# A first product by 49 block products instead of seven, in groups of 2048 tokens

## The chip, the cores and the metric

The kernel runs on one core of one Trainium2 chip. The metric is the time of one execution on the device in microseconds (us). Three runs of the kernel before took 2756.13 to 2757.7 us, median 2757.11. The profiled execution is a run of its own and took 2755.91 us.

## The reference

`x` is 32 batches of 128 tokens with 2048 features, in float32. Two residual layers follow one another; each batch chooses its adapter by one id per layer.

```
# layer 0: dense weight for all batches, and a rank-16 adapter chosen per batch (8 adapters)
base  = einsum('bsi,oi->bso', x, W0) + bias
low   = einsum('bsi,bri->bsr', x, a[id0])
delta = einsum('bsr,bor->bso', low, b[id0])
x = x + base + scale[id0] * delta
# layer 1: a whole 2048 x 2048 weight chosen per batch out of 16
x = x + einsum('bij,bkj->bik', x, W1[id1])
```

Both layers are 4096 x 2048 x 2048 products in float32.

## The kernel before

Each float32 operand is split into two fp32r parts, `hi` (a rounding copy on ACT, line 574) and `lo` = value minus `hi` (a subtraction on DVE with both inputs in SBUF, line 710), and each product is three matmuls: hi·hi, hi·lo and lo·hi (lines 766, 767, 777 in the first product; 820 to 822 in the second). The residual is an identity matrix that POOL adds to the weights (lines 486 and 493).

The batches are sorted by their id of layer 1 on the chip. Four groups g of 1024 tokens (two halves of 512) go through both products one after the other. The first product of a group is done by seven block products k instead of eight, at one level, on quarters of weight and tokens: half of the outputs by half of the inputs, 8 tiles each way. For each k the operands are sums or differences of quarters. They are made in the ring `raw` of eight 4 KB tiles: SP loads the pieces (`raws_of` gives them), POOL adds them in place (line 476, 128x1024), eight sums of the weight fall to DVE (line 644). Sums of W0 are written to memory in group 0 and read back in groups 1 to 3, one sum of x is kept per group. A `W` block (g, k, o) is one output tile: 8 input tiles times three matmuls of 512 columns, 24 in all, into one of three PSUM banks in turn. DVE (for k = 0 ACT, line 543) takes the bank and adds it into up to two of the four result quarters `cb` (lines 687 to 704, 128x512 out of PSUM). So of DVE's large instructions some have two inputs in SBUF (line 710), and some have one in PSUM (lines 687 to 704).

`LA` blocks are the adapter's first product (16 matmuls), with the adapter's second product in the `W` blocks of k = 2, 3, 5 (line 775) and as `LB` after those of k = 6 (line 787).

The second product is streamed: per half, 512 output columns and 256 inputs there are three `S` blocks of 12, 6 and 6 matmuls, each with its tile of W1 (4 KB a partition, split as above). ACT copies the result out, SP stores it.

What sets the order: `plan_blocks` writes TensorE's order down. From it, with a price per block (`COST`, 0.2267 us a matmul), planned start and end times are summed, each split and eviction gets a key out of these times, and the sorted keys are the order on ACT, DVE, POOL and SP. Each engine then goes through its list in order and waits by semaphores. POOL's instructions stand in the order of the splits that they serve; SP issues every load and store, and a load into a ring place waits until the split of what lay there is done.

## Time and profile before

| | |
|---|---|
| three runs, median (lowest to highest) | 2757.11 us (2756.13 to 2757.7) |
| the profiled execution, its own time | 2755.91 us |
| its span in the profile | 2754.1 us |
| TensorE clock granted | 0.999 |
| busy: PE, DVE, ACT, POOL | 99%, 67%, 49%, 27% |
| DMA share of the span | 69% |

PE is TensorE's matmul side. The busy shares are unions of the recorded instructions of an engine over the span; an instruction that has begun and is held up is recorded as busy, so a mean over all instructions of a line mixes undisturbed and held ones.

### The profile page before, as it was taken

What the parts mean: (1) busy time and instruction counts of PE and PEld (TensorE: products, weight loads), DVE (VectorE), ACT (ScalarE), POOL (GpSimd) and SP (SyncE); (2) the same over time, 40 slices, a digit from 0 to 9 for tenths busy, and PEclk for the clock granted to TensorE, in tenths of its full rate; (3) what the DMA queues carried; (4) which work ended last, traced back from release to release, by engine and by line L of the source; (5) the groups of instructions that cost most, each with busy time, mean ns of one, the idle gap of its engine ahead of it and who ended that gap; (6) DMA issues with size and microseconds to landing.
All of it is one profiled execution on the core that took longest, in us unless ns stands there. A gap on an engine that the chain in (4) does not pass through costs nothing.

```text
span 2754.1 us, 34174 instructions
## 1 busy us (share of the span) xinstructions
PE 2713.4 (99%) x12042; PEld 2244.8 (82%) x12042; DVE 1836.7 (67%) x1631; ACT 1339.2 (49%) x1409; POOL 732.9 (27%) x589
## 2 busy tenths in 40 slices
PE   6999999999999999999999999999999999999999
PEld 5788888888888888888888888888888888888887
DVE  5766776866655657686656575768675656667865
ACT  3332355756533335576643232666664323366665
POOL 4435812411512111141251210113134122111421
PEclk9999999999999999999999999999999999999999
DMA  7858947666855435666794544899997554499997
GB/s 269 331 188 284 351 167 225 206 222 219 312 173 198 143 129 178 211 221 208 232 310 161 185 156 137 288 305 312 308 326 276 168 180 163 138 303 311 309 321 246
DMA packets 197627, 645.17 MB, mean 234 GB/s; under 512 B 23216, under 2 KB 33616, under 8 KB 197456
## 3 DMA queue, kind: packets, MB, share of 16 engines
q1 hardware_dynamic: 197456, 642.98, 68.6%
q8 instruction: 96, 1.57, 0.2%
q14 instruction: 75, 0.61, 0.1%
HBM read 651.28 MB, written 58.72 MB: 258 GB/s over the span
## 4 chain that ended last, share of the span: by engine, by line
PE 89%; POOL 3%; DMA 3%; DVE 3%; ACT 1%; issue 1%; SPq 0%; POOLq 0%; ACTq 0%; DVEq 0%
PE acc L820 16%; PE acc L821 16%; PE acc L822 16%; PE acc L766 13%; PE acc L777 13%; PE acc L767 13%; DMA raw<-w 3%; POOL raw L493 2%; PE acc L739 2%; DVE ws L710 1%; POOL raw L476 1%; PE acc L775 1%; DMA raw<-xt 0%; DVE ops L710 0%; ACT ws L574 0%
## 5 line engine op out<-in xcount | busy, mean ns | idle before, releaser
L710 DVE TENSOR_TENSOR ws<-raw,ws 128x1024 fp32r<-128x1024 f32 (+1 forms) x1008 | 1317.5, 1330 | 432.9 <-ACT ws L574 428.8
L574 ACT CAST ws<-raw 128x1024 fp32r<-128x1024 f32 (+1 forms) x1008 | 1027.9, 1044 | 1146.7 <-PE acc L777 519.0
L820 PE MATMUL acc<-ws,ops 128*128 128x512 f32 (+1 forms) x2048 | 799.0, 390 | 5.2 <-DVE ws L710 4.8
L821 PE MATMUL acc<-ws,ops 128*128 128x512 f32 (+1 forms) x2048 | 797.9, 390 | 0.0
L822 PE MATMUL acc<-ws,ops 128*128 128x512 f32 (+1 forms) x2048 | 797.9, 390 | 0.0
L766 PE MATMUL acc<-ops,ws 128*128 128x512 f32 x1792 | 702.1, 392 | 19.8 <-DVE ops L710 14.4
L777 PE MATMUL acc<-ops,ws 128*128 128x512 f32 x1792 | 700.9, 391 | 0.0
L767 PE MATMUL acc<-ops,ws 128*128 128x512 f32 x1792 | 699.8, 391 | 0.0
L493 POOL TENSOR_TENSOR raw<-raw,eye_s 128x128 f32<-128x128 f32 x384 | 351.6, 946 | 1261.3 <-DMA raw<-w 1261.3
L820 PEld LDWEIGHTS acc<-ws,ops 128*128 128x128 f32 x2048 | 384.6, 188 | 89.1 <-issue 6.5
L476 POOL TENSOR_TENSOR raw<-raw 128x1024 f32<-128x1024 f32 (+1 forms) x116 | 305.6, 2636 | 555.1 <-DMA raw<-xt 456.5
L822 PEld LDWEIGHTS acc<-ws,ops 128*128 128x128 f32 x2048 | 384.6, 188 | 79.5
L821 PEld LDWEIGHTS acc<-ws,ops 128*128 128x128 f32 x2048 | 384.7, 188 | 78.6
L766 PEld LDWEIGHTS acc<-ops,ws 128*128 128x128 f32 x1792 | 338.0, 189 | 88.0 <-DVE ops L710 14.6
L767 PEld LDWEIGHTS acc<-ops,ws 128*128 128x128 f32 x1792 | 337.9, 189 | 69.6
L777 PEld LDWEIGHTS acc<-ops,ws 128*128 128x128 f32 x1792 | 337.5, 188 | 67.7
L710 DVE TENSOR_TENSOR ops<-raw,ops 128x1024 fp32r<-128x1024 f32 x112 | 171.8, 1534 | 68.2 <-ACT ops L574 67.6
L574 ACT CAST ops<-raw 128x1024 fp32r<-128x1024 f32 x112 | 117.3, 1048 | 180.9 <-PE acc L777 85.6
L710 DVE TENSOR_TENSOR ops<-cb,ops 128x1024 fp32r<-128x1024 f32 x64 | 84.0, 1312 | 0.0
L486 POOL TENSOR_TENSOR raw<-raw,eye_s 128x128 f32<-128x128 f32 x80 | 68.4, 863 | 57.8 <-DMA raw<-w 56.4
L692 DVE SCALAR_TENSOR_TENSOR cb<-acc,bias_s,cb 128x512 f32<-128x512 f32 x32 | 24.0, 751 | 85.8 <-PE acc L777 85.8
L574 ACT CAST ops<-cb 128x1024 fp32r<-128x1024 f32 x64 | 67.1, 1048 | 13.8 <-PE acc L777 13.8
(61 smaller groups left out, 651.4 us busy)
## 6 DMA issues: line engine op xcount, KB each, us to landing
raw<-w SPq DMA_DIRECT2D x928, 512.0 KB
raw<-xt SPq DMA_DIRECT2D x176, 512.0 KB
raw<-w_sums SPq DMA_DIRECT2D x104, 512.0 KB
out<-ost SPq DMA_DIRECT2D x128, 256.0 KB, 6.0
w_sums<-raw SPq DMA_DIRECT2D x32, 512.0 KB, 5.3
x_sums<-raw SPq DMA_DIRECT2D x16, 512.0 KB, 4.2
raw<-x_sums SPq DMA_DIRECT2D x16, 512.0 KB
raw<-a SPq DMA_DIRECT2D x80, 64.0 KB
```

The costliest lines, as they stand in the source:

```text
L476: eng.tensor_tensor(b, b, a, ALU.subtract if step == "sub" else ALU.add).then_inc(s_pool, 1)
L486: eng.tensor_tensor(v, v, eye_s[:], ALU.add).then_inc(s_pool, 1)
L493: ins = eng.tensor_tensor(v, v, eye_s[:], ALU.add)
L574: ins = eng.copy(hi, src)
L710: ins = eng.tensor_tensor(lo, src, hi, ALU.subtract) if hi is not None else eng.tensor_copy(lo, src)
L739: ins = eng.matmul(acca[:], a_view(n)[:, t, :], ops[:, h + t, w, :], start=(i % 2 == 0 and t == 0 and w == 0), stop=(i % 2 == 1 and t == H ...
L766: eng.matmul(acc, wh, xh, start=(t == 0), stop=False)
L767: eng.matmul(acc, wh, xl, start=False, stop=False)
L777: ins = eng.matmul(acc, wl, xh, start=False, stop=(t == HT - 1))
L820: eng.matmul(acc, yh, wh, start=begin, stop=False)
L821: eng.matmul(acc, yh, wl, start=False, stop=False)
L822: ins = eng.matmul(acc, yl, wh, start=False, stop=end)
```

## The change

There are now two groups of 2048 tokens (four quads q of 512), and the first product has two levels. The outer seven products k are on halves as before; each is again done by seven products s, whose operands are 512 inputs by 512 outputs by 512 tokens. A block `W` (g, k, s, b) is two output tiles of 4 input tiles each, again 24 matmuls of 512 columns, into a pair of PSUM banks; there are 7 x 7 x 2 = 98 blocks per group, where one level on 1024 tokens had 56. The pairs of s = 2, 3 and 4 go on adding into the pair that s = 1 began, and s = 6 into that of s = 5 (`more`), so that the sums of a chain build up in PSUM; DVE (ACT for four of seven s at k = 0 and 3) takes the pair after every s, 128x1024, and the next block into that pair waits for it. Two pairs alternate.

Operands: for each k, four quarters r of each side in two halves h lie in SBUF as 128x1024 tiles, in ten places a side. Level-one sums (`Xform`, `Wform`) are added there by POOL, 512 columns at a time, from four small tiles `temps`: two per tile of x for k = 2, one for k = 3, 4 and 5; in group 0 also one per tile of the weight for k = 3, 5 and 6. Level-two sums are made by POOL out of these, in place: T3, T2, T4, T1 of x and S3, S2, S4, S1 of the weight, each for both h and every k, 128x1024. The quarters of k+1 are loaded into the places of k as its splits finish. DVE makes the weight sum of k = 2 at the start, in eight times two additions. Every operand of s is split, 14 tiles of x and 14 of weight per k, 128x1024 each. The finished result quarters go to memory (`keep`, `ystore`) and some come back (`back`, and `Y` loads); POOL adds kept ones in (`join`, 128x1024, eight at k = 3 and eight at k = 5). `LA` blocks are 16 of 8 matmuls per group; `LB` is apart from the `W` blocks, in bursts of four 256-column matmuls, each followed by two additions of 512 columns on DVE. Three operand slots of the weight instead of four. The second product has the same blocks as before, two groups of 768; its ring has ten places. POOL and SP now have lists of their own, sorted by planned times that `Plan` works out: it gives an addition of 128x1024 2.7 us, a load 3.5 us and a split 2.8 us, and does not let the instructions of an engine queue behind one another.

```diff
--- before.py
+++ after.py
@@ -11,229 +11,500 @@
...
-HT = 8
 G = 4
-NG = 4
-NQ = 8
+NG = 2
+NQ = 4
...
+X_ROLE = (0, 1, 4, 3, 0, 1, 2)
+W_ROLE = (0, 1, 4, 2, 3, 1, 0)
+X_NEXT = (4, 3, 0, 1, 2)
+W_NEXT = (4, 2, 3, 1, 0)
+X_QUARTER = ((1, 0), (0, 0), (1, 1), (0, 1))
+W_QUARTER = ((0, 1), (0, 0), (1, 0), (1, 1))
+BLOCK = ((0, 0), (0, 0), (0, 1), (1, 1), (1, 0), (1, 1), (0, 1))
+EARLIER = {1: 0, 5: 3, 6: 2}
+FINAL = {(0, 0): 1, (0, 1): 6, (1, 1): 5, (1, 0): 4}
+LORA_K = (0, 1, 3, 6)
+LORA_S = (0, 1, 3, 6)
+COPY_S = (0, 2, 3, 4)
+FINAL_K = (1, 4, 6)
+LB_AT = {(0, 0, 0): (1, ((2, 1), (3, 0))), (0, 1, 0): (2, ((1, 0), (1, 1))),
+         (0, 0, 1): (2, ((2, 1), (3, 0))), (0, 1, 1): (3, ((1, 0), (1, 1))),
+         (1, 0, 0): (4, ((2, 1), (3, 0))), (1, 1, 0): (5, ((1, 0), (1, 1))),
+         (1, 1, 1): (5, ((2, 0), (2, 1))), (1, 0, 1): (5, ((3, 0), (3, 1)))}
+LB_LATE = [(c, i, j) for c in (2, 3) for j in range(2) for i in range(2)]
 
 
 def plan_blocks():
...
+        for k in range(NP):
+            for s in range(NP):
+                for b in range(2):
+                    blocks.append(("W", g, k, s, b))
+                    if b == 0 and k in LORA_K and s in LORA_S:
+                        blocks.append(("LA", g, k, s))
+                    if (k, s, b) in early:
+                        blocks.append(("LB", g) + early[k, s, b])
+        for q in range(NQ):
             for kc in range(C1):
                 for u in range(NU):
                     for j in range(3):
-                        blocks.append(("S", g, h, kc, u, j))
-                        if held:
-                            blocks += held
-                            held = []
...
+def form_steps(side, g, k):
+    if side == "X":
+        return (0, 0, 2, 1, 1, 1, 0)[k]
+    return 1 if g == 0 and k in (3, 5, 6) else 0
+
+
+def saved_here(side, g, k):
+    return k == 2 if side == "X" else g == 0 and k in (3, 5, 6)
+
+
+def eye_here(g, k):
+    return k in (0, 4) or (g == 0 and k in (3, 5))
+
+
...
+        ready, free = [], []
+        for h in range(2):
+            slot = 2 * at[g, k][r] + h
+            before[g, k, r, h] = saves[slot]
+            fill[slot] += 32 if side == "X" and k in (0, 1, 2, 6) else 16
+            landed[g, k, r, h] = fill[slot]
+            t = when[h]
+            if (g, k) == (0, 0):
+                t = 18.0 + 0.01 * r + 0.001 * h if side == "X" else 0.01 * r + 0.001 * h
+            elif (g, k, side) == (0, 2, "W"):
+                t = max(t, self.early_done + 6.0)
+            self.sync.append((t, (side + "load", g, k, r, h)))
+            t += LOAD
+            for step in range(form_steps(side, g, k)):
+                done = t
+                for l in range(2):
+                    use = (side, g, k, r, h, l, step)
+                    done = max(self.take_temp(use, 1, t - LOAD + 0.2 * l, 1), done)
+                    what = (side + "form", g, k, r, h, l, step)
+                    self.pool.append((done, what))
+                    done += ADD / 2
+                    self.give_temp(use, 1, done, ("pool", what))
+                t = done
+            if side == "W" and r in (1, 3) and eye_here(g, k):
+                self.pool.append((t, ("eye", g, k, r, h)))
+                t += 1.2
+            ready.append(t)
+            if saved_here(side, g, k):
+                saves[slot] += 16
...
+            for h in range(2):
+                t3 = max(x_ready[2][0][h], x_ready[3][1][h])
+                t2 = max(t3 + ADD, x_ready[1][0][h], x_free[4][h])
+                xs[h] = (t3, t2)
+                self.pool += [(t3, ("T3", g, k, h)), (t2, ("T2", g, k, h))]
+                s3 = max(w_ready[1][0][h], w_ready[2][1][h])
+                s2 = max(s3 + ADD, w_ready[3][0][h], w_free[4][h])
+                wsum[h] = (s3, s2)
+                self.pool += [(s3, ("S3", g, k, h)), (s2, ("S2", g, k, h))]
+            have_x = {0: x_ready[0][0], 1: x_ready[1][0], 2: [xs[h][1] + ADD for h in range(2)],
...
+                for h in range(2):
+                    key = max(free + 0.3 + 3.0 * h, have_x[s][h])
+                    self.splits.append((key, "X", (g, k, s, h)))
+                    done.append(key + SPLIT)
+                xd[s] = done
+                if s < 2:
+                    for h in range(2):
+                        t = max(xs[h][1] + ADD, done[h], x_ready[s][1][h])
+                        self.pool.append((t, ("T4" if s == 0 else "T1", g, k, h)))
...
+        def pair_of(s, b):
+            return pair[((1, 2), (0, 1), (0, 1), (0, 1), (0, 1), (2, 0), (2, 0))[s][b]]
...
+                    z21, z11, z22, z12, v = (x_view(g, k, r, h) for r in range(5))
+                    if kind == "T3":
+                        wait_x(eng, g, k, 2, h)
+                        wait_x(eng, g, k, 3, h)
+                        wait_saved(eng, "X", g, k, 3, h)
+                        ins = eng.tensor_tensor(z12, z22, z12, ALU.subtract)
+                    elif kind == "T2":
+                        eng.wait_ge(s_pool, pool_no["T3", g, k, h])
+                        wait_x(eng, g, k, 1, h)
+                        wait_x_free(eng, g, k, 4, h)
+                        ins = eng.tensor_tensor(v, z12, z11, ALU.add)
+                    elif kind == "T4":
+                        eng.wait_ge(s_pool, pool_no["T2", g, k, h])
+                        eng.wait_ge(s_lo, number["X", g, k, 0, h] + 1)
+                        wait_saved(eng, "X", g, k, 0, h)
+                        ins = eng.tensor_tensor(z21, z21, v, ALU.subtract)
+                    else:
+                        eng.wait_ge(s_pool, pool_no["T2", g, k, h])
+                        eng.wait_ge(s_lo, number["X", g, k, 1, h] + 1)
+                        wait_saved(eng, "X", g, k, 1, h)
+                        ins = eng.tensor_tensor(z11, z22, v, ALU.subtract)
+                    ins.then_inc(s_pool, 1)
...
+                    if kind == "Xform" and k in (2, 3):
+                        ins = eng.tensor_tensor(t, t, other, ALU.add if step else ALU.subtract)
+                    elif kind == "Wform" and k == 5:
+                        ins = eng.tensor_tensor(t, t, other, ALU.add)
+                    else:
+                        ins = eng.tensor_tensor(t, other, t, ALU.subtract)
...
+                elif kind == "join":
+                    _, g, k, i, j, b = what
+                    m = 2 * (2 * i + j) + b
+                    if k == 3:
+                        eng.wait_ge(s_keep[m], 16 * (g + 1))
+                        wait_ev(eng, g, 3, FINAL[i, j], b)
+                        wait_ev(eng, g, 2, FINAL[i, j], b)
+                    else:
+                        eng.wait_ge(s_back[m], 16 * (g + 1))
+                        wait_ev(eng, g, 5, FINAL[i, j], b)
...
+            elif kind == "X":
+                g, k, s, h = index
+                m = 4 * ((NP * k + s) % 2)
+                v = x_view(g, k, X_ROLE[s], h).rearrange("p (l t c) -> p l t c", l=2, t=4)
+                hi, lo = (ops[:, m:m + 4, w, 256 * h:256 * h + 256].rearrange("p t (l c) -> p l t c", l=2)
+                          for w in range(2))
...
+                if what == "copy":
+                    g, k, s, b = index
+                    i, j = BLOCK[s]
+                    if k == 0 and g:
+                        eng.wait_ge(s_lo, max(number["Y", g - 1, 3, u] for u in range(NU)) + 1)
+                    if k == 3:
+                        eng.wait_ge(s_y[2 * (2 * i + j) + b], 32 * g + 16)
+                    eng.wait_ge(s_mm, at["W", g, k, s, b] + 1)
+                    eng.copy(cube(1 if k == 0 else 0, i, j, b), pair_of(s, b)[:]).then_inc(s_copy, 1)
...
+                if what == "ev":
+                    g, k, s, b = index
+                    i, j = BLOCK[s]
+                    which = 0 if k in (1, 3, 4) else 1
+                    t = cube(which, i, j, b)
+                    if s in EARLIER:
+                        wait_ev(eng, g, k, EARLIER[s], b)
+                    elif k == 1:
...
+                    eng.wait_ge(s_mm, at["W", g, k, s, b] + 1)
+                    source = cube(1, i, j, b) if k == 1 and s not in EARLIER else t
+                    eng.tensor_tensor(t, pair_of(s, b)[:], source, ALU.add).then_inc(s_ev, 1)
                     continue
...
+                    _, g, k, s, b = blk
+                    n, m = (14 * k + 2 * s + b) % NWS0, 4 * ((NP * k + s) % 2)
+                    if b == 0:
+                        eng.wait_ge(s_lo, max(number["X", g, k, s, h] for h in range(2)) + 1)
...
+                    if s == 0 and k:
+                        wait_ev(eng, g, k - 1, 6 if b else 4, 0 if b else 1)
+                    elif s == 0 and g:
+                        eng.wait_ge(s_ev1, out_no(g - 1, NQ * C1 - 2, 3 if b else 1) + 1)
+                    elif s == 1 and b:
+                        wait_ev(eng, g, k, 0, 0)
+                    elif s == 1 and k:
+                        wait_ev(eng, g, k - 1, 6, 1)
+                    elif s == 1 and g:
+                        eng.wait_ge(s_ev1, out_no(g - 1, NQ * C1 - 1, 1) + 1)
+                    elif s == 5 and b:
+                        wait_ev(eng, g, k, 4, 0)
+                    elif s == 5:
+                        wait_ev(eng, g, k, 0, 1)
+                        for burst in bursts:
...
+                    more = s in (2, 3, 4, 6)
+                    for o in range(2):
+                        acc = pair_of(s, b)[:, 512 * o:512 * o + 512]
+                        for t in range(4):
+                            c = P * (4 * o + t)
+                            wh, wl = ws0[:, n, 0, c:c + P], ws0[:, n, 1, c:c + P]
+                            xh, xl = ops[:, m + t, 0, :], ops[:, m + t, 1, :]
+                            eng.matmul(acc, wh, xh, start=(t == 0 and not more), stop=False, skip_group_check=more)
+                            eng.matmul(acc, wh, xl, start=False, stop=False, skip_group_check=more)
+                            ins = eng.matmul(acc, wl, xh, start=False, stop=(t == 3), skip_group_check=more)
                     ins.then_inc(s_mm, 1)
                 else:
```

## Rows read from the trace of the kernel before

**Rows 1.** The page: span, and busy us (share) and instructions of each engine.
```profile
span 2754.1 us, 34174 instructions
...
PE 2713.4 (99%) x12042; PEld 2244.8 (82%) x12042; DVE 1836.7 (67%) x1631; ACT 1339.2 (49%) x1409; POOL 732.9 (27%) x589
```
**Rows 2.** TensorE's waits: engine, line, released by: us in total, times, longest.
```profile
PE acc L766 <- DVE ops L710: 14.4, 1, 14.4
PE acc L766 <- DVE ws L710: 5.2, 4, 1.7
PE acc L820 <- DVE ws L710: 4.8, 5, 1.6
```
**Rows 3.** Windows: from:to, length, busy us (instructions) per engine, TensorE clock, DMA share, GB/s.
```profile
24.00:362.00 338.00, 329.89 (x1458) 271.71 (x1458) 231.56 (x210) 109.51 (x113) 182.45 (x96) 0.99 0.79 282
362.00:711.00 349.00, 347.53 (x1534) 287.24 (x1533) 253.72 (x208) 220.93 (x233) 82.34 (x85) 1.00 0.65 215
711.00:1040.00 329.00, 329.00 (x1478) 273.11 (x1477) 193.77 (x191) 113.26 (x120) 72.53 (x50) 1.00 0.53 182
```
**Rows 4.** The chain that ended last: start us, us, what.
```profile
759.09 3.63 PE acc L739 x16
...
944.58 7.25 PE acc L739 x32
```
**Rows 5.** Instructions grouped by form: count | busy us, mean ns | idle before.
```profile
L710 DVE TENSOR_TENSOR ws<-raw,ws 128x1024 fp32r<-128x1024 f32 x992 | 1303.8, 1337 | 431.4 <-ACT ws L574 427.6
...
L766 PE MATMUL acc<-ops,ws 128*128 128x512 f32 x1792 | 702.1, 392 | 19.8 <-DVE ops L710 14.4 <-DVE ws L710 5.2
...
L476 POOL TENSOR_TENSOR raw<-raw 128x1024 f32<-128x1024 f32 x112 | 300.5, 2684 | 524.6 <-DMA raw<-xt 456.5 <-DMA raw<-w 66.2 <-POOL raw L476 0.4
...
L710 DVE TENSOR_TENSOR ops<-raw,ops 128x1024 fp32r<-128x1024 f32 x112 | 171.8, 1534 | 68.2 <-ACT ops L574 67.6
...
L702 DVE TENSOR_TENSOR cb<-acc,cb 128x512 f32<-128x512 f32 x32 | 22.1, 691 | 75.2 <-PE acc L777 75.2
...
L476 POOL TENSOR_TENSOR raw<-raw 128x512 f32<-128x512 f32 x4 | 5.2, 1292 | 30.5 <-DMA raw<-a 30.5
```
**Rows 6.** Timeline of DVE, 198 to 209 us: start, us, engine, line, instruction.
```profile
199.19 1.21 DVE L710 TENSOR_TENSOR ops<-raw,ops 128x1024 fp32r<-128x1024 f32 x1
200.32 3.42 DVE L710 TENSOR_TENSOR ws<-raw,ws 128x1024 fp32r<-128x1024 f32 x1
204.22 0.75 DVE L692 SCALAR_TENSOR_TENSOR cb<-acc,bias_s,cb 128x512 f32<-128x512 f32 x1 [0.48 <-PE acc L777]
204.89 2.62 DVE L710 TENSOR_TENSOR ws<-raw,ws 128x1024 fp32r<-128x1024 f32 x1
```
**Rows 7.** Timeline of POOL in the same stretch.
```profile
199.85 2.81 POOL L476 TENSOR_TENSOR raw<-raw 128x1024 f32<-128x1024 f32 x1 [5.04 <-DMA raw<-w]
202.74 1.32 POOL L486 TENSOR_TENSOR raw<-raw,eye_s 128x128 f32<-128x128 f32 x1
204.03 2.40 POOL L476 TENSOR_TENSOR raw<-raw 128x1024 f32<-128x1024 f32 x1
```
**Rows 8.** Timeline: the first matmul of the first product.
```profile
23.67 0.80 PE L766 MATMUL acc<-ops,ws 128*128 128x512 f32 x1 [14.44 <-DVE ops L710]
```
**Rows 9.** SP's timeline: the first loads of weight and of x.
```profile
2.60 0.90 SPq L423 DMA_DIRECT2D raw<-w  x2
11.80 0.88 SPq L431 DMA_DIRECT2D raw<-xt  x2
```
**Rows 10.** Windows again: the first stretch after that matmul.
```profile
24.00:75.00 51.00, 49.90 (x210) 40.74 (x210) 32.84 (x31) 16.99 (x22) 31.94 (x16) 1.00 0.85 310
```
**Rows 11.** The page's DMA issues: count, KB each, median us from issue to landing.
```profile
out<-ost SPq DMA_DIRECT2D x128, 256.0 KB, 6.0
...
x_sums<-raw SPq DMA_DIRECT2D x16, 512.0 KB, 4.2
```
**Rows 12.** The chain that ended last again: two loads in it.
```profile
49.23 5.69 DMA raw<-xt
...
99.54 7.35 DMA raw<-w
```

More of the change, by code:

```diff
@@ new lines, in x_piece, with w_piece @@
+            def x_piece(g, iq, quad, lane):
+                src = xt[bass.ds(order(NQ * g + quad, 0)[lane], 1), iq]
+                return src.rearrange("a p n -> (a p) n")
+            def w_piece(k, r, h):
+                ro, co = {0: (0, 0), 1: (0, 1), 4: (1, 1)}[k]
+                ri, ci = W_QUARTER[r]
+                return w0[2 * ro + ri, 2 * co + ci, h]
+            constants = False
+            for _, what in plan.sync:
+                kind = what[0]
+                if not constants and kind == "Xload":
+                    constants = True
@@ L506, in split_views @@
             if kind == "Y":
[L507 to L516 removed]
+                g, q, u = index
```

1465 lines of the change are left out of this document (939 added, 526 removed).

## Prediction

> **What bounds the kernel now.** I read the busy shares first: TensorE 2713.4 us of a span of 2754.1 [rows 1]. Its waits come to little: 14.4 us for the first operands, then pieces of about 5 us [rows 2]. The windows say the same by stage: 329.89 of 338 us in group 0's first product, 347.53 of 349 in its second, 329.00 of 329 in group 1's first [rows 3]. So TensorE is the bound and everything else fits beneath it; a change that takes matmuls out pays only while that stays so. The question is what the others need per block afterwards.
>
> Two prices of TensorE: 16 matmuls of 512 columns in 3.63 us and 32 in 7.25 [rows 4], 0.2267 us each. A W block is 24 of them, 5.44 us.
>
> **What POOL and DVE do to each other** decides this case. The means are 2684 ns for POOL's 128x1024 addition and 1337 or 1534 for DVE's lo subtraction [rows 5]; the timelines show what is in them. DVE's subtraction from 199.19 ends at 200.40. POOL's addition had begun at 199.85 and ends at 202.66, 2.26 after that. DVE's next began at 200.32 and ends at 203.74, 1.08 after POOL. POOL's 128-wide addition ends at 204.06, 0.32 after DVE. And DVE's subtraction from 204.89 ends at 207.51, 1.08 after POOL's 206.43 [rows 6, 7]. Each waits for the other to finish, instruction by instruction: the two share something that one holds at a time, for 1.08 us (DVE, 1024 wide), 2.26 (POOL, 1024) and 0.32 (POOL, 128). Undisturbed they record about 1.21 and 2.40, as some 0.15 at the ends is free. An eviction out of PSUM is not part of it: 0.75 us from 204.22, wholly inside POOL's 204.03 to 206.43, and neither is longer than alone [rows 6, 7].
>
> The Trainium skill says why (SBUF — State Buffer, "SBUF: two separate sides"): DVE and GpSimd share a port pair as an exclusive lock held for the whole instruction, and a DVE operation takes part when it has two SBUF inputs. By that rule the sum below adds the two engines; if they ran side by side it would be the first rival's. The trace agrees with the rule in every number of the paragraph above.
>
> **The change, part by part.**
>
> TensorE. Before, 4 x 56 W blocks of 24 = 5376 matmuls (1792 on each of three lines, rows 5); now 2 x 98 x 24 = 4704. LA stays at 256 of 512 columns, LB at 256 of 256, the second product at 6144. Gone: 672 x 0.2267 = 152.3 us.
>
> Per outer product k TensorE now has 14 blocks, 336 matmuls, 76.2 us; plus 7.3 for four LA blocks at k = 0, 1, 3, 6, and 0.9 for each LB item (8 half-width matmuls, estimated at half price). Together 77 to 84 us, 569 per group.
>
> The shared resource. POOL's 512-wide addition is nowhere seen being released by DVE; between 0.32 (128) and 2.26 (1024) a straight line gives 1.15, an estimate; 1.29 as recorded [rows 5] is the upper end. For each k:
> - level-two sums: 8 kinds x 2 halves = 16 of 2.26 = 36.2 us
> - lo subtractions: 14 of x, 14 of weight = 28 of 1.08 = 30.2 us
>
> That is 66.4 us for every k, under TensorE's 77. What comes on top, for the products k that have it: x formed from temps, 32 halves at k = 2 (36.8), 16 at k = 3, 4, 5 (18.4); weight formed in group 0, 16 halves at k = 3, 5, 6 (18.4); eight joins of 2.26 from k = 3, falling on k = 4, and eight from k = 5, falling on k = 6 (18.1); identities, 8 of 0.32 at k = 0, 4 and in group 0 at 3, 5 (2.6); adapter operands, 2 to 5 for LA, 1.7 per LB item (1 to 3 of them at k = 1 to 5). At k = 0 of group 0 also DVE's 16 additions of weight (17.3). The sums, lock against TensorE:
> - group 0: k = 0: 89/83, 1: 71/84, 2: 107/78, 3: 111/84, 4: 107/77, 5: 111/79, 6: 108/83
> - group 1: k = 0: 71/83, 1: 71/84, 2: 107/78, 3: 90/84, 4: 107/77, 5: 90/79, 6: 89/83
>
> The places of k+1 come free only as k's splits go through, so POOL can work about one k ahead and no more; the slack of k = 0 and 1 is not carried to later ones. From k = 2 on TensorE waits for the difference: 142 us in group 0, 81 in group 1, together 223. Bounds: if all slack could be carried, the difference of the totals, 702 + 625 − 1139 = 189; with the undisturbed durations (1.21, 2.40, 1.29, 0.46) in place of the held ones the same table gives 319. I take 223, since under pressure the two alternate and the held durations are what counts.
>
> The start. Eight weight halves and six early ones, 7.3 MB, are issued ahead of x; at 310 GB/s [rows 10] 24 us from SP's first load at 2.6 [rows 9], then 1 MB of x, 3.4 us, and the splits, 2.5: first matmul near 32 instead of 23.67 [rows 8]. LA's operand queues behind all of x (4 MB, 13 us) and arrives some 7 us after it is due. Between 0 (if SP gets x out earlier) and 25; I take 15.
>
> Coupling. A slot's new content can only be asked for after the split of the old: SP, then 4.2 to 7.35 us to land [rows 11, 12]. In a phase without slack POOL idles for about one such gap: 10 phases x 4.5 = 45. And TensorE's next s needs one eviction and three lo subtractions after the last block of s−2; with POOL's additions between them 1.4 + 3 x (1.08 + 2.26) = 11.4 us, and ACT's 1.05 ahead, against 10.9 of cover. That costs about 1.5 us per s where POOL is busy but not the bound, say 5 in all. Sum 50, between 0 and 150.
>
> At nothing: the pair of PSUM banks that must be emptied before its next block. An eviction of 128x1024 (two of the 0.69 of rows 5, so 1.2 to 1.4 us) has 5.44 us of cover by the other pair's block; before, two blocks covered it. Queued behind it on DVE are the next s's splits; its cover goes when lo subtractions ahead of it are held, and that is counted in coupling. ACT's 28 copies of 1.05 and up to 8 evictions per k stay near 40 of 77 us. DMA: per k from 2 on some 20 to 25 MB in 107 us or more, 190 to 235 GB/s, under the 310 it moves at [rows 10]. The second product per u is as before; its windows show TensorE busy 347.53 of 349 with POOL at 82 and DVE at 254 [rows 3]; LB's late bursts and the loads of Y go beside it. Two changes of group fewer give back nothing, since the windows show none of them costly.
>
> Sum against the profiled execution's own time: 2755.9 − 152.3 + 223 + 15 + 50 = 2891.6; the median of the runs is 1.2 above that execution, so 2893 us.
>
> **Rivals.**
>
> *TensorE stays the bound (faster).* POOL's own work per group, at its undisturbed durations, is about 500 us in group 0 and 430 in group 1 against 569, and DVE's about 70%; each fits alone. If the lock's instructions always found the other engine idle or evicting, only the start would be lost: 2757 − 152 + 15 = 2620. For: both look idle on the page (27% and 67%). Against: the release times above, and that the sums over 100 us leave no room for it. It decides where the lock's sum per k is under 80. 5%.
>
> *Nearly carried.* POOL gets far enough ahead in k = 0, 1 and during the second product, the start is hidden and coupling is nil: 2605 + 189 = 2794, down to 2760 if also a third of TensorE's old waits (some 38 us in all, rows 1) and the forming of half-tiles come cheaper. 8%, a quarter of it within 0.2% of before.
>
> *Alternation sets the pace (slower still).* DVE takes its list in order, so an eviction, and with it TensorE's next block, stands behind lo subtractions that each wait for a whole POOL addition: per s 4 x (1.08 + 2.26) + 2 x 1.2 = 15.8 us where POOL always has a full addition ready, and about 12.9, with one full and one half hold less, at k = 0 and 1. The 70 steps of k = 2 to 6 then take 1106 us and 45 for their LA and LB, 1151 against the 1027 of my table; the 28 others 56 more. With the refill gaps of 45 and without the 5: 2893 + 124 + 56 − 5 = 3068. It decides from one full addition ready per subtraction on. For: a 1.21 us subtraction that took 3.42 [rows 6]. Against: from k = 2 on most of what POOL has ready is half wide, so its holds are shorter. 12%.
>
> The forecast itself: 75%.
>
> **Range and chances.** The forecast's own terms reach from 2805 (223 down to 189, start 5, coupling 10) to 3030 (start 20, coupling and longer holds 120 more). That leaves about 1 in 10 on each side. A difference under 0.2%, 5.5 us, is what a measurement of this kernel can't tell from none. Faster 0.06, same 0.02, slower 0.92.
>
> **What would show it.** In the changed trace: 11370 matmuls; TensorE busy 2560 or so, under 90% of the span; its waits led by lo subtractions of the first product; windows of k = 2 to 6 in group 0 over 100 us, of k = 1 near 84; POOL without long idle there, waiting for DVE and DMA little; DVE's lo subtractions with a mean of 1.8 us or more in the first product, evictions near 1.2; group 0's first product about 60 us longer than group 1's; the second product's windows unchanged at 349 us per 1536 matmuls. The forecast is wrong if TensorE has its 5.44 us pitch of blocks through k = 2 to 5, or if POOL idles long in them while TensorE waits, which would put the loads or the order of a queue in the lock's place.

## The result: 3036 us, slower by a tenth, and where it went

The changed kernel took 3035.93 us (median of four runs, 3030.13 to 3036.99) against 2757.22: ratio 1.1007, 95% interval 1.0988 to 1.1026. The direction was forecast, the size was not: +279 us instead of +136, and 3036 lies outside the range (2805 to 3030).

The page of the changed kernel, its head and part 1, beside [rows 1]:

```profile
span 3035.0 us, 35105 instructions
...
PE 2659.0 (88%) x11370; PEld 2172.5 (72%) x11370; DVE 2244.2 (74%) x1747; ACT 1395.5 (46%) x1481; POOL 1536.3 (51%) x929
```

TensorE's longest waits in the changed kernel (us in total, times, longest), beside [rows 2]:

```profile
PE acc L1342 <- DVE lb L1312: 180.2, 19, 34.0
PE pair L1369 <- DVE cb L1307: 46.8, 4, 28.8
PE pair L1404 <- DVE cb L1307: 38.2, 11, 6.2
PE pair L1404 <- DVE ops L1312: 37.4, 8, 26.1
```

TensorE's busy time and the sum of all its waits close the account; these are the four longest lines of eleven. The waits sum to 371.7 us against 36.7 before (eight lines): +335.0. Its busy time is 2659.0 where 2713.4 − 152.3 = 2561.1 was due for 11370 matmuls: +97.9. And −152.3 + 335.0 + 97.9 = 280.6; the spans differ by 280.9. Half of the waits, 180.2 us, end at line 1342, the LA blocks: they wait for the split of a 256-column adapter operand, up to 34 us at a time. The forecast had 288 us of waits and no lower clock, so of the 145 us that it fell short, 47 are waits and 98 are the busy time.

Windows of the changed kernel over the first product of group 0, cut at the first W block of k = 2, 3, 4, 5 and 6, and the second product of group 0 (length, busy us of PE, PEld, DVE, ACT, POOL; clock, DMA share, GB/s), beside [rows 3]:

```profile
264.00:368.00 104.00, 87.15 (x352) 70.43 (x351) 89.52 (x66) 31.98 (x32) 92.72 (x47) 0.90 0.60 203
368.00:516.00 148.00, 90.91 (x377) 73.64 (x377) 68.25 (x45) 38.18 (x42) 124.92 (x70) 0.82 0.43 146
516.00:606.00 90.00, 82.11 (x347) 67.10 (x346) 77.71 (x49) 30.02 (x30) 77.76 (x40) 0.94 0.67 229
606.00:731.00 125.00, 86.59 (x360) 70.63 (x359) 86.77 (x60) 34.06 (x34) 95.39 (x48) 0.84 0.59 211
731.00:850.00 119.00, 87.42 (x367) 71.33 (x366) 68.30 (x67) 34.77 (x38) 60.33 (x39) 0.86 0.22 70
858.00:1584.00 726.00, 710.93 (x3124) 583.90 (x3124) 550.88 (x457) 454.21 (x483) 198.81 (x192) 0.99 0.68 221
```

Forecast for these k: 107, 111, 107, 111, 108. They took 104, 148, 90, 125, 119. k = 2 and 4, which have no LA block, are at or under the forecast. k = 3 and 6, which have four, are 37 and 11 us over it. So are the first two, which also have four: k = 0 took 117 us (35.4 to 152.8 in the trace) and k = 1 took 111 (to 263.9), where TensorE's own time is 83 and 84. And so is k = 5, with no LA block but with LB's bursts, one of which waited 28.8 us (below). That k = 4 is 17 under says that POOL used k = 3's long stops to work ahead: it is recorded busy 124.92 and 77.76 us in the two, 202.7 together. The mean of TensorE's clock is 0.82 to 0.94 in these windows. The second product of group 0 took 733 us from its first matmul at 851.1, where 705 are due (two windows of 349 before and 7 for LB's late blocks); the waits stand at its two ends. It took 722 in experiment 6 too, so most of this isn't from the two causes below.

The changed kernel's groups of the lo subtractions, evictions and POOL's sums (count | busy us, mean ns | idle before), beside [rows 5]:

```profile
L1312 DVE TENSOR_TENSOR ops<-stage,ops 128x1024 fp32r<-128x1024 f32 x160 | 342.6, 2175 | 7.4 <-ACT ops L1167 7.2
...
L928 POOL TENSOR_TENSOR stage<-stage,temps 128x512 f32<-128x512 f32 x80 | 146.6, 1853 | 64.3 <-DMA temps<-xt 64.1
...
L980 POOL TENSOR_TENSOR wq<-wq 128x1024 f32<-128x1024 f32 x28 | 86.6, 3093 | 11.7 <-DVE ws L1312 6.4 <-issue 5.4
...
L1307 DVE TENSOR_TENSOR cb<-pair,cb 128x1024 f32<-128x1024 f32 x164 | 199.6, 1217 | 67.9 <-PE pair L1406 67.0
```

What the prediction called the shared resource is there: the subtraction of x has a mean of 2175 ns instead of 1534, a POOL sum of 1024 columns in the kind shown 3093 (2.8 to 3.2 us over the eight kinds), one of 512 columns 1853, and the eviction out of PSUM 1217, untouched.

One of the stops. The timeline of ACT in the changed kernel (start, us, engine, line; in brackets the idle time before and what ended it):

```profile
227.82 1.05 ACT L1167 CAST ws<-wq 128x1024 fp32r<-128x1024 f32 x1 [2.49 <-PE pair L1406]
253.75 0.40 ACT L1167 CAST lb<-temps 128x256 fp32r<-128x256 f32 x1 [24.88 <-POOL temps L1003]
```

The timeline of POOL over the same stretch:

```profile
225.27 10.25 POOL L928 TENSOR_TENSOR stage<-stage,temps 128x512 f32<-128x512 f32 x5
...
248.26 2.34 POOL L970 TENSOR_TENSOR wq<-wq 128x1024 f32<-128x1024 f32 x1
...
252.99 0.72 POOL L1003 TENSOR_TENSOR temps<-temps 128x256 f32<-128x256 f32 x1
```

That of SP's queue of loads:

```profile
248.46 0.33 SPq L813 DMA_DIRECT2D temps<-xt  x1
248.99 2.23 SPq L824 DMA_DIRECT2D temps<-a  x4
```

And that of TensorE at the end of the stop:

```profile
254.66 3.78 PE L1342 MATMUL acc<-ops,lb 128*128 128x512 f32 x8 [16.06 <-DVE lb L1312]
258.24 0.60 PE L1404 MATMUL pair<-ops,ws 128*128 128x512 f32 x1
...
258.92 0.40 PE L1406 MATMUL pair<-ops,ws 128*128 128x512 f32 x1
259.15 0.39 PE L1404 MATMUL pair<-ops,ws 128*128 128x512 f32 x1
```

The window of those eight matmuls of the LA block:

```profile
254.66:258.24 3.58, 3.58 (x8) 2.81 (x9) 3.58 (x3) 3.29 (x4) 3.22 (x2) 0.50 0.59 220
```

ACT's next item is an adapter split. It stands idle for 24.88 us until POOL has added the operand (252.99, 0.72 us long). From 225.27 on POOL was at sums of the next k, all but one of them level-one, which stand ahead in its list; the operand itself was asked for only at 248.99, as SP's list holds it behind loads into `temps` that wait for POOL to free one. ACT's next four splits (254.06 to 257.95) then went through without a wait, so what held them was their place behind this one: TensorE waited for 256 columns. The last two fences show what a stop costs besides itself: the eight matmuls from 254.66 to 258.24 ran at a granted clock of 0.50, that is 1.2 GHz, and are 0.447 us apart; those from 258.92 on are 0.23 apart.

The other adapter operand, that of LB, does the same at k = 5. ACT and TensorE in the changed kernel:

```profile
640.18 2.10 ACT L1167 CAST lb<-temps 32x1024 fp32r<-32x1024 f32 x2 [30.78 <-DMA temps<-bt]
651.48 1.19 PE L1369 MATMUL pair<-lows,lb 128*128 128x256 f32 x4 [28.80 <-DVE cb L1307]
```

ACT stood for 30.78 us before the split of LB's operand, whose load had been issued only at 636.60. DVE stood behind ACT, and the eviction that LB's block needs came after both.

### The profile page after: what moved, and what is told of

It reads as the page before. It is cut to its first block and busy times, and to the rows that moved or that the text cites. A ratio compares the mean times of both kernels' runs of the same rounds, so it can differ in the third digit from the quotient of the medians.

```text
span 3035.0 us, 35105 instructions
## 1 busy us (share of the span) xinstructions
PE 2659.0 (88%) x11370; PEld 2172.5 (72%) x11370; DVE 2244.2 (74%) x1747; ACT 1395.5 (46%) x1481; POOL 1536.3 (51%) x929
## 5 line engine op out<-in xcount | busy, mean ns | idle before, releaser
L1312 DVE TENSOR_TENSOR ws<-wq,ws 128x1024 fp32r<-128x1024 f32 x964 | 1297.7, 1371 | 341.0 <-ACT ws L1167 335.9
L1167 ACT CAST ws<-wq 128x1024 fp32r<-128x1024 f32 x964 | 986.9, 1050 | 1051.0 <-PE pair L1406 501.7
L1024 POOL TENSOR_TENSOR wq<-wq,eye_s 128x128 f32<-128x128 f32 x384 | 377.5, 1015 | 1050.9 <-DMA wq<-w 1050.8
L1404 PE MATMUL pair<-ops,ws 128*128 128x512 f32 x1568 | 635.6, 405 | 76.2 <-DVE cb L1307 38.2
L1405 PE MATMUL pair<-ops,ws 128*128 128x512 f32 x1568 | 630.7, 402 | 0.0
L1406 PE MATMUL pair<-ops,ws 128*128 128x512 f32 x1568 | 627.3, 400 | 0.0
L1439 PE MATMUL pair<-ws,yops 128*128 128x512 f32 (+1 forms) x1536 | 601.2, 391 | 13.5 <-DVE ws L1312 13.5
L1440 PE MATMUL pair<-ws,yops 128*128 128x512 f32 (+1 forms) x1536 | 599.9, 391 | 0.0
L1441 PE MATMUL pair<-ws,yops 128*128 128x512 f32 (+1 forms) x1536 | 599.3, 390 | 0.0
L1404 PEld LDWEIGHTS pair<-ops,ws 128*128 128x128 f32 x1568 | 308.6, 197 | 149.9 <-issue 42.1
L1406 PEld LDWEIGHTS pair<-ops,ws 128*128 128x128 f32 x1568 | 306.8, 196 | 67.0
L1405 PEld LDWEIGHTS pair<-ops,ws 128*128 128x128 f32 x1568 | 308.3, 197 | 64.1
L1312 DVE TENSOR_TENSOR ops<-stage,ops 128x1024 fp32r<-128x1024 f32 x160 | 342.6, 2175 | 7.4 <-ACT ops L1167 7.2
L1439 PEld LDWEIGHTS pair<-ws,yops 128*128 128x128 f32 x1536 | 289.7, 189 | 77.3 <-issue 13.5
L1441 PEld LDWEIGHTS pair<-ws,yops 128*128 128x128 f32 x1536 | 289.5, 188 | 61.0
L1440 PEld LDWEIGHTS pair<-ws,yops 128*128 128x128 f32 x1536 | 289.6, 189 | 58.5
L1307 DVE TENSOR_TENSOR cb<-pair,cb 128x1024 f32<-128x1024 f32 x164 | 199.6, 1217 | 67.9 <-PE pair L1406 67.0
L1342 PE MATMUL acc<-ops,lb 128*128 128x512 f32 x256 | 89.3, 506 | 180.3 <-DVE lb L1312 180.2
L1439 PE MATMUL acc<-ws,yops 128*128 128x512 f32 (+1 forms) x512 | 201.8, 394 | 15.1 <-DVE ws L1312 15.0
```

What stands on the lines that cost most here:

```text
L1024: ins = eng.tensor_tensor(v, v, eye_s[:], ALU.add)
L1167: ins = eng.copy(hi, src)
L1307: eng.tensor_tensor(t, pair_of(s, b)[:], source, ALU.add).then_inc(s_ev, 1)
L1312: ins = eng.tensor_tensor(lo, src, hi, ALU.subtract) if hi is not None else eng.tensor_copy(lo, src)
L1342: ins = eng.matmul(acc, lora_view(blk)[:, t, :], ops[:, m + t, w, :], start=(begin and t == 0 and w == 0), stop=(end and t == 3 and w == 1))
L1404: eng.matmul(acc, wh, xh, start=(t == 0 and not more), stop=False, skip_group_check=more)
```

## The experiments

Theory *lock*: POOL's additions and DVE's subtractions exclude each other, and their sum sets the pace of k = 2 to 6. Theory *order*: the adapter's operands stand at places of the lists that were planned without queues, come late, and stop ACT, DVE and TensorE. Ratios are to the kernel before.

### 1. No adapter operands: 2877.45 us, 1.0437 (1.0416 to 1.0458)

```diff
             free = lora_done[-2] if len(lora_done) >= 2 else now - 30.0
             key = max(free + 0.2, soon - 9.0)
...
+            if (g, k) != (0, 0) or s > 1:
+                lora_there[k, s] = now - 20.0
+                return
...
-                            if blk[5] == 0:
+                            if blk[5] == 0 and blk[1:5] == (0, 0, 0, 0):
```

> The changed kernel without the adapter's operands: all LA and LB matmuls stay, but only the first two LA operands and the first LB operand of the first product are loaded, added and split; later ones read those again. Theory order: the adapter's small additions stand in POOL's list behind the level-one sums of the next k, their splits stand in ACT's and DVE's lists ahead of everything else, and the whole kernel stops for them; these waits (183 us at LA, 82 at LB) and the lower clock after them go, so 2780 to 2830 us. Theory lock: the stops only hide the shared resource, which then shows in their place at k = 3, 5 and 6; 2850 to 2950 us, with k = 2 and 4 unchanged near 104 and 90 us.

Above order's range and inside lock's: the adapter was worth 158 us, and other waits show in its place. Of the spans' difference of 160 us, 124 are TensorE's waits and 35 its busy time. The waits at LA fall by 176 us (180.2 to 4.2), while those at W blocks rise from 76.0 to 101.0 and those at LB from 79.6 to 106.2. So LB's waits aren't gone with its operands. The stop at k = 5 is there again, by another cause; ACT and TensorE in experiment 1:

```profile
589.65 1.04 ACT L1170 CAST ws<-wq 128x1024 fp32r<-128x1024 f32 x1 [26.18 <-POOL wq L973]
604.22 1.19 PE L1374 MATMUL pair<-lows,lb 128*128 128x256 f32 x4 [25.37 <-DVE cb L1279]
```

ACT waits for a level-two sum. DVE has nothing to do for 21.92 us before 590.73, and POOL's 1024-wide additions from 568.62 to 589.58 take 2.33 to 2.40 us, the undisturbed time: there it is not the exclusion that holds TensorE but POOL's own list, which is late. Windows of experiment 1, k = 2 to 6 of group 0 and k = 0 to 4 of group 1 (columns as above):

```profile
243.00:341.00 98.00, 81.53 (x355) 67.18 (x354) 73.02 (x54) 28.03 (x28) 93.20 (x47) 0.91 0.58 204
341.00:450.00 109.00, 88.42 (x379) 72.61 (x378) 74.74 (x38) 35.49 (x36) 103.38 (x53) 0.91 0.56 200
450.00:556.00 106.00, 83.42 (x343) 67.66 (x343) 77.77 (x46) 28.09 (x28) 105.13 (x51) 0.89 0.48 170
556.00:670.00 114.00, 84.50 (x363) 69.52 (x362) 84.42 (x55) 27.99 (x28) 95.50 (x49) 0.87 0.66 247
670.00:772.00 102.00, 88.57 (x368) 72.02 (x367) 81.55 (x64) 33.78 (x34) 73.50 (x36) 0.93 0.24 88
1507.00:1592.00 85.00, 84.63 (x370) 70.06 (x371) 62.92 (x35) 36.30 (x39) 62.68 (x23) 0.99 0.32 106
1592.00:1677.00 85.00, 84.41 (x377) 69.90 (x376) 81.67 (x63) 27.97 (x28) 75.07 (x34) 1.00 0.61 211
1677.00:1778.00 101.00, 81.56 (x354) 67.20 (x353) 78.09 (x55) 28.00 (x28) 95.26 (x43) 0.90 0.50 187
1778.00:1866.00 88.00, 85.49 (x375) 70.58 (x375) 75.62 (x39) 35.28 (x36) 87.86 (x38) 0.98 0.55 197
1866.00:1969.00 103.00, 84.04 (x349) 68.56 (x348) 77.92 (x46) 28.11 (x29) 102.71 (x43) 0.90 0.39 148
```

This is the prediction's table, less its adapter terms of 2 to 5 us, in a trace: 98, 109, 106, 114, 102 where it says 103, 106, 105, 106, 103; and 85, 85, 101, 88, 103 where it says 83, 84, 103, 85, 105. Not in the fence, and further off: k = 0 and 1 of group 0 took 115 and 93 us, and k = 5 and 6 of group 1 took 89 and 94, where the table less its adapter terms has about 85 for each. POOL is recorded busy 103.38 of 109 and 105.13 of 106 us where the sum is highest.

### 2. Adapter operands asked for earlier: 3073.85 us, 1.1143 (1.1124 to 1.1162)

```diff
-            key = max(free + 0.2, soon - 9.0)
+            key = free + 0.2
...
-                upcoming = (k, s + 1) if s < 6 else (k + 1, 0)
-                if upcoming[0] in LORA_K and upcoming[1] in LORA_S:
-                    lora(*upcoming, now + 6.0)
+                while upcoming_lora:            # as soon as LA n-2 is done
+                    lora(*upcoming_lora.pop(0), now)
```

> The changed kernel with the adapter's operands asked for as soon as their slot is free (LA two blocks ahead, LB one burst ahead) instead of about 9 and 12 us before they are due by the plan; nothing left out. Theory order: nearly all of e1's gain, 2790 to 2850 us, ACT's waits for POOL's adapter additions (348 us) under 60. Theory lock: 2860 to 2960 us. If both are wrong and temps are too few, 3036 or more.

A miss: 38 us slower than the changed kernel, 16 of them before its first matmul. The waits at LA are nearly gone from TensorE (5.4 us), and have moved. Waits of all engines in experiment 2, ACT's and TensorE's longest:

```profile
ACT lb L1180 <- POOL temps L1014: 224.2, 10, 49.5
...
PE pair L1417 <- DVE ops L1325: 148.0, 14, 41.8
...
PE pair L1417 <- DVE cb L1320: 117.9, 20, 38.0
ACT lb L1180 <- POOL temps L1016: 117.9, 8, 27.2
```

The edit moved the load, the addition and the split together. The split now stands earlier in ACT's list too and waits there just as long for POOL's additions (the two ACT lines, 342.1 us, against 347.8 in the changed kernel), in front of W blocks' operands instead of LA's. Earlier isn't the remedy as long as POOL and `temps` serve it no sooner. A version that loads and adds earlier but keeps the split late was not tried, so the part of place alone isn't isolated.

### 3 and 5. Level-two sums as fills that read nothing

2822.99 us, 1.0239 (1.0219 to 1.0260), with one fill of 1.80 us; 2875.23 us, 1.0428 (1.0406 to 1.0450), with two that take 1.34 + 1.02.

```diff
-                        ins = eng.tensor_tensor(z12, z22, z12, ALU.subtract)
+                        ins = eng.memset(z12.bitcast(mybir.dt.bfloat16), 0.5)               # 3
+                        eng.memset(z12[:, 0:748].bitcast(mybir.dt.bfloat16), 0.5)           # 5
+                        ins = eng.memset(z12[:, 748:1024].bitcast(mybir.dt.uint8), 63)
```

(and so for all eight kinds; the first line after the minus is experiment 3, the other two are experiment 5)

> The changed kernel with each of POOL's 224 level-two sums replaced by a fill of the same tile that reads nothing (operands wrong from then on, all else the same). Theory lock: if a fill that reads no SBUF isn't held against DVE's subtractions, their mean in the first product falls from 2.1 us to 1.5 or less, and k = 2 to 6 lose 20 to 30 us each even if the fill takes as long as the addition; 2800 to 2880 us. Theory order: POOL's backlog shrinks only if the fill is shorter; the stops at LA stay above 120 us in all.

> As the third experiment (POOL's 224 level-two sums replaced by fills that read nothing), but with two fills per sum, one of 1496 two-byte and one of 1104 one-byte elements, so that POOL is occupied about as long as by an undisturbed addition (2.3 to 2.4 us against 2.40; the fill before took 1.80). Theory lock: what DVE's subtractions wait for is not POOL's being busy but its reading of SBUF beside them; the fills are never lengthened and the time stays near the third experiment's 2823, 2820 to 2880 us. Theory POOL capacity (POOL is simply too full): the gain of the third experiment came from the shorter fill, and most of it is lost again, 2930 us or more.

POOL's fills in experiment 5, grouped by form:

```profile
L975 POOL MEMSET wq<- 128x1496 bf16 x28 | 37.6, 1345 | 0.2
...
L976 POOL MEMSET wq<- 128x1104 uint8 x28 | 28.5, 1018 | 0.0
```

DVE's subtraction of x in the same trace:

```profile
L1320 DVE TENSOR_TENSOR ops<-stage,ops 128x1024 fp32r<-128x1024 f32 x160 | 239.0, 1525 | 10.1 <-ACT ops L1175 9.6
```

A pair of fills takes 1345 + 1018 = 2363 ns, as long as an undisturbed sum (2.40, [rows 7]), against 2.8 to 3.2 us for the sums they replace. With POOL occupied as long, but reading nothing, the mean of the subtraction of x fell from 2175 to 1525 ns and the kernel by 161 us. So it is not POOL's being busy that holds DVE's subtractions, but its reading. For a DVE operation with two SBUF inputs the Trainium skill limits the exclusion to a GpSimd operation that reads SBUF (SBUF — State Buffer, "SBUF: two separate sides"). These fills agree. The 52 us between 3 and 5 are POOL's own time: a longer fill delays the adapter's additions behind it (TensorE's wait at LA 107.3 and 133.0 us, and 180.2 with sums).

### 4 and 6. Short level-two sums, alone and without adapter operands

2766.77 us, 1.0040 (1.0025 to 1.0055), and 2637.96 us, 0.9567 (0.9548 to 0.9586).

```diff
-                        ins = eng.tensor_tensor(z12, z22, z12, ALU.subtract)
+                        ins = eng.tensor_tensor(z12[:, 0:128], z22[:, 0:128], z12[:, 0:128], ALU.subtract)
```

(and so for all eight kinds; only T2 and S2 of the very first k keep their width)

> The changed kernel with POOL's level-two sums 128 columns wide instead of 1024 (most of the columns are then not summed). The shared resource needs 31 us less for every k and is under TensorE's time for all. Theory lock: k = 2 to 6 at 80 to 88 us, 2650 to 2720 us. Theory order: POOL's backlog is gone too, so most stops go, but the plan's just-in-time loads of the adapter operands stay late at k = 1, 3 and 6: 2720 to 2800 us.

> Both together: no adapter operands after the first (as e1) and 128-column level-two sums (as e4). If the shared resource and the adapter's place in the lists are the two causes, TensorE is the bound again but for the start: 2604 + 12 for the start + 20 to 50 = 2635 to 2670 us, clock 0.99. If something else still stops it (PSUM pairs that wait for their eviction, loads), 2700 or more.

| us | adapter operands | without |
|---|---|---|
| sums 1024 wide | 3035.9 | 2877.5 |
| sums 128 wide | 2766.8 | 2638.0 |

The wide sums cost 239 to 269 us, the adapter's operands 129 to 158; each makes the other dearer by 30. The 269 are not all exclusion: experiment 5, where POOL is occupied as long and DVE isn't held, stands between at 2875.2, so 161 us are the exclusion and 108 are POOL's own time in its in-order list. With both causes out, TensorE is the bound again. The page of experiment 6:

```profile
span 2636.9 us, 34109 instructions
...
PE 2572.5 (98%) x11370; PEld 2122.4 (80%) x11370; DVE 1983.5 (75%) x1687; ACT 1358.1 (52%) x1421; POOL 1057.5 (40%) x901
```

Windows of k = 2 to 4 of group 0 in experiment 6 (columns as above):

```profile
219.00:297.00 78.00, 78.00 (x353) 64.85 (x352) 65.49 (x50) 27.95 (x28) 59.95 (x47) 1.00 0.77 272
297.00:381.00 84.00, 84.00 (x375) 69.65 (x375) 55.84 (x38) 35.32 (x36) 78.72 (x63) 1.00 0.65 244
381.00:458.00 77.00, 77.00 (x345) 63.89 (x344) 69.44 (x46) 28.04 (x28) 68.90 (x42) 1.00 0.73 255
```

78, 84 and 77 us are TensorE's own times of the prediction's table, at full clock. The block's one-block cover of its PSUM eviction, three operand slots instead of four, the loads and the stores stop nothing in these windows; whether they would beside full sums isn't shown. 2638 is the 2604 that the fewer matmuls give and 34 us for the start (28.9 instead of 23.7 us, and 99 and 91 us for k = 0 and 1 of group 0) and the edges of the second products.

### 7, 8, 10, 11. Sums on DVE, and other prices in the plan

Nothing is left out in these. 7: level-two sums on DVE, 2948.43 us, 1.0687 (1.0669 to 1.0705). 8: level-one sums too, 2975.98, 1.0794 (1.0776 to 1.0812). 10: only the weight's level-two sums, with the plan's prices changed, 2950.52, 1.0706 (1.0688 to 1.0724). 11: as 7 with those prices, 2862.06, 1.0385 (1.0368 to 1.0402).

```diff
+MOVED = ('T1', 'T2', 'T3', 'T4', 'S1', 'S2', 'S3', 'S4')     # 8: and Xform, Wform; 10: S1 to S4
...
+    for key, what in plan.adds:
+        vector_tasks.append((key, len(vector_tasks), "add", what))
...
-LOAD = 3.5
-ADD = 2.7
-SPLIT = 2.8
+LOAD = 5.0      # 10 and 11
+ADD = 3.6
+SPLIT = 3.6
```

> The changed kernel with the level-two sums (T1 to T4, S1 to S4) on DVE instead of POOL, in DVE's list at the same planned times; nothing left out. Theory lock: each holds the shared resource 1.08 us instead of 2.26, 18.9 us less for every k; k = 2 to 6 sum to 88, 92, 88, 92, 89 in group 0, and POOL's backlog before the adapter's additions shrinks by 38 us per k: 2790 to 2870 us. If DVE as the one in-order list is what counts, its 18 us more per k make evictions later: 2950 us or more.

> As e7, and the level-one sums (Xform, Wform) on DVE too; POOL keeps the adapter's additions, identities and joins. Held sum at most 47.5 + 18 + 20 = 85 us for any k, DVE busy up to 93 of them. Theory order: with nothing ahead of them in POOL's list the adapter's additions are no longer late, so most of the 183 us at LA go: 2740 to 2830 us. If DVE's list now waits for loads of temps with evictions behind, 2850 or more.

> Only the weight's level-two sums (S1 to S4) on DVE, those of x stay on POOL, and the plan with an addition at 3.6 us, a load 5.0, a split 3.6. Held sum per k 9.4 us less than in the changed kernel: k = 2 to 6 at 97, 102, 98, 101, 98 in group 0. Theory lock plus order: 2870 to 2950 us, below the 2948 of all sums on DVE, as evictions have fewer additions ahead of them. If DVE's list is the bound: 2950 or more.

> All level-two sums on DVE as in the seventh experiment (2948 us), with the plan of the tenth. There TensorE waits 148 us for evictions that stand in DVE's list behind sums that aren't ready. Theory order: with the sums placed later these fall under 80 us, 2840 to 2900 us. If the additions' place isn't the cause, 2930 to 2970.

TensorE's longest waits in experiment 7:

```profile
PE pair L1420 <- DVE cb L1323: 147.9, 17, 28.8
PE pair L1420 <- DVE ops L1328: 66.1, 14, 30.2
PE acc L1358 <- DVE lb L1328: 31.8, 9, 7.2
```

And in experiment 11:

```profile
PE pair L1420 <- DVE ops L1328: 88.7, 16, 29.2
PE acc L1358 <- DVE lb L1328: 54.6, 8, 15.4
PE pair L1420 <- DVE cb L1323: 45.8, 12, 15.5
```

7 came 88 us below the changed kernel, less than lock alone gives and 2 us under what was expected with DVE's list as the new trouble: the shared resource is lighter and POOL's backlog gone (LA's waits 180.2 to 31.8 us), but sums that aren't ready now stand in DVE's list ahead of evictions, 147.9 us. 11 changes only places in the lists and wins 86 us; the waits for evictions fall to 45.8. 8, with the level-one sums on DVE as well, is 28 us slower than 7: taking POOL's last large sums away gained nothing. 10 differs from 11 in leaving the sums of x on POOL, and is 88 us slower.

### 9. Other prices alone: 3011.40 us, 1.0931 (1.0913 to 1.0949)

```diff
-LOAD = 3.5
-ADD = 2.7
-SPLIT = 2.8
+LOAD = 5.5
+ADD = 4.5
+SPLIT = 4.0
```

> The changed kernel with other prices in its plan, which alone decide the order of the lists: an addition 4.5 us instead of 2.7, a load 5.5 instead of 3.5, a split 4.0 instead of 2.8, nearer to what they take with their waits. Nothing else differs. Theory order: the adapter's operands now stand where TensorE really needs them relative to the sums of the next k, so part of the 265 us of waits at LA and LB goes: 2900 to 2980 us. Theory lock alone: the order is worth nothing, 3020 to 3050 us.

25 us, less than order expected, and the waits at LA stay (179.7 us). So do TensorE's waits as a whole (372.5 us against 371.7); what fell is its busy time, from 2659.0 to 2632.2. In this plan an engine's items don't queue, so POOL's backlog of one k isn't in it at any price. That this is why dearer prices moved so little was argued and not tested.

### 12. Experiment 11 without adapter operands: 2806.08 us, 1.0188 (1.0171 to 1.0205)

```diff
 (the edits of 11 and of 1)
-                    if len(registers) >= 5:
+                    if len(registers) >= 3:
```

> The eleventh experiment (all level-two sums on DVE, slower prices in the plan, 2862 us) without the adapter's operands after the first, as in the first experiment; also SP keeps three instead of five sets of batch numbers in registers. It says what is left when the adapter no longer stops anything and the additions hold the shared resource half as long. Theory lock and order as the two causes: 56 us of waits at LA, 17 at LB and some 15 of slow clock go: 2765 to 2800 us, and the kernel stays slower than the one before because DVE's single list now carries sums, splits and evictions. If the waits at W blocks (139 us) were themselves caused by late adapter splits ahead of them, under 2750.

56 us, above the range given. Left are waits of 193 us in all, most at W blocks for DVE's splits of x (92.1, of which 28.8 before the first matmul) and evictions (63.3). No version with the whole computation came under the kernel before; 11, 4% slower, is the nearest.

## Why the prediction was right in direction and wrong in size

The slowdown and its two main parties were forecast; the size failed at two steps, the adapter's operands (in *coupling*) and TensorE's clock (not in the sum). What was lost beyond TensorE's own times of the prediction's table, by stage, slow clock included:

| us lost | forecast | changed | exp. 1 | exp. 6 |
|---|---|---|---|---|
| before the first matmul, beyond 23.7 | 8 | 12 | 12 | 5 |
| k = 0 and 1, both groups | 7 | 96 | 43 | 24 |
| k = 2 to 6, both groups | 273 | 312 | 202 | 4 |
| both second products, beyond 705 each | 0 | 42 | 44 | 30 |

(The kernel before loses some 28 us of the same kinds, so a column is not yet the difference to it.)

**TensorE's saving**, −152.3: right; 11370 matmuls, and experiment 6 has them at 77 to 84 us per k.

**The shared resource**, +223: the exclusion and the held times were right, the price is right only roughly. Experiment 1 has the k of its fence within 8 us of the table; their excess over TensorE's own time from k = 2 on is about 200 us in both groups, slow clock included. Experiment 5 shows the exclusion with POOL's occupation kept: 161 us. But the table is a sum of two engines that both always have work, and that isn't what happens throughout: at k = 5 DVE idles for 22 us while POOL works undisturbed. POOL's own time as one worker with one list is a second price, 108 us between experiments 5 and 4, which the prediction had only as part of the sum. That the sum came near is in part luck.

**The start**, 15: right in size, but not for the reason given. The first matmul came at 35.4 instead of 23.67 us, and LA waited 4.4. The first tile of x was there by 24.9 us, not near 30. DVE then split three tiles of x in 9.96 us beside POOL's sums of the weight; with fills in place of the sums the first matmul comes at 28.3 and 28.9. So 6 to 7 of the 11.7 us are the shared resource.

**Coupling**, 50: this term failed, with the line before it that gave LA's operand 7 us at the start and nothing later. I counted the adapter's operands by their work, 2 to 5 us per k, and not by their places. They stand in POOL's list behind the next k's sums, in SP's behind `temps`, and in ACT's and DVE's ahead of every other split. A POOL that is at its limit makes them late by its backlog, 12 to 34 us at the seven longest stops, and nothing passes them. Measured: 180.2 us of TensorE's waits at LA instead of 7, another 28.8 at the LB block of k = 5, and 158 us in the time (experiment 1). The waits elsewhere were fewer than forecast, 155 us more than before instead of 281, since while TensorE stands at LA it doesn't stand for the sums; that the waits as a whole came within 47 us of the 288 is two errors that nearly cancel. The refill gaps that made up 45 of the 50 were not measured apart. Their lower end, 4.2 us, was also read from a store [rows 11]; the loads shown take 5.69 and 7.35 [rows 12].

**TensorE's clock**, at nothing in the sum and without a reason, though the sum's waits were there: +97.9 us of busy time, the largest single part of the 145 that were missing. Over the first products the mean granted clock was 0.82 to 0.94 in every k but one (0.99 at k = 0 of group 1), between its levels of 1.2 and 2.4 GHz. After the stop at 254.66 eight matmuls took 3.6 us instead of 1.8. It goes with the stops: busy time beyond 2561.1 is 97.9 us with 371.7 of waits, 62.5 with 247.3 (experiment 1) and 11.4 with 60.6 (experiment 6), and between 0.18 and 0.30 of the waits in all thirteen traces of the new kernel. It isn't a fixed share: 372.5 us of waits cost 71.1 in experiment 9. Priced at what experiment 1 shows, a quarter of the waits, the 288 us that I forecast would have become 360, and 2965 us, without any new cause, within the range given.

**The range** was added up loosely: its terms give about 2809 and 3018, not 2805 and 3030. The measured time is above both.

**The rivals.** *TensorE stays the bound* needed the lock's sum under 80 and failed where it said. Its 2620 is met at 2638 only with both causes taken out. *Alternation sets the pace*, 3068, is nearest in time and not the cause: without adapter operands it asks for 111 us in each k from 2 on, and they took 98 to 114 in group 0, which does not tell it from the sum, but 101, 88, 103, 89 and 94 in group 1; and k = 2 and 4 took 104 and 90 even with the operands. *Nearly carried* fell: no slack was carried from k = 0 and 1, which lost time themselves.

Open: the clock's loss was read from the traces and never isolated; why experiment 2's start came 16 us later was not followed; and what a late LB operand costs by itself, since in experiment 1 the waits at LB rose to 106.2 us without it.

## What to carry to other kernels

Add up what two engines hold in common before asking whether each has room: POOL at 27% and DVE at 67% looked idle and were over the limit together once POOL's additions doubled and more. A small operand that passes through the same in-order lists as the big ones costs its place, not its length: find what stands ahead of it on the engine that makes it, and what stands behind it on the next. And in these traces TensorE's stops cost a fifth to three tenths more than themselves, so a forecast with waits in it needs a clock in it.

## What the runs showed of the hardware that was not expected

- POOL's fill of 128x2048 two-byte elements takes 1.80 us beside DVE's subtractions as well as alone, while its 128x1024 addition, 2.40 alone, has means of 2.8 to 3.2 us by kind. Six of the 224 fills in experiment 3 took 2.35, and each of the six began while a copy on DVE was recorded (one input in SBUF, 32x1024, 1.15 to 1.98 us instead of 0.69).
- The release is the same each time. In the trace before, 58 subtractions stand by themselves and end after a POOL addition that they overlap, and all end 1.07 to 1.09 us after it; 29 POOL additions of 1024 columns end after a subtraction in the same way, all 2.24 to 2.27 us after it. The longest subtraction takes 3.46 us and the longest addition 3.42, each one's own time and one hold of the other: neither was passed over twice.
- A 256-column subtraction on DVE (0.42 us alone) had a mean of 1385 ns in the changed kernel, and 558 with the fills of experiment 5: it is the other's instruction, not its own length, that sets what a short one pays.
